# Three of eight k tiles of the state-space output projection as fp32r products of high and low parts

## The reference, cut to what matters

```python
y = ys.transpose(1, 0, 2, 3) + D[None, None, :, None] * xh
y = y.reshape(b, l, D_INNER)                      # D_INNER = 1024
y = y * jax.nn.silu(z)                            # the gated output
y = y * jax.lax.rsqrt(jnp.mean(y * y, axis=-1, keepdims=True) + EPS) * norm_w
return y @ W_out.T                                # 1024 -> 512, the output projection
```

## Time and profile before

| | |
|---|---|
| median of 3 runs | 2111.36 us (2105.56, 2112.68, 2111.36) |
| profiled execution, its own time | 2112.64 us |
| its span in the trace | 2110.9 us |
| state-space stage | about 0 to 905 us of the span |
| PE, DVE, ACT, POOL busy over the span | 94%, 69%, 58%, 18% |
| TensorE clock granted, mean | 0.972 of full speed |

### The profile page before, as it was taken

The page is one execution under the profiler, slowest core; times in us unless marked ns, Lnnn a source line. Parts: engine busy times, 40 slices in busy tenths (PEclk is TensorE's granted clock), DMA queues, the critical chain, the costliest instruction groups (busy, mean ns, idle before and its releaser), DMA issues. The chain is left out here.

```text
span 2110.9 us, 40225 instructions
## 1 busy us (share of the span) xinstructions
PE 1974.6 (94%) x13484; PEld 1328.5 (63%) x13484; DVE 1453.8 (69%) x2889; ACT 1221.2 (58%) x3068; POOL 390.2 (18%) x597
## 2 busy tenths in 40 slices
PE   7899999999999999858999999999999999889988
PEld 5667675768676767444565656656656655478853
DVE  7978787878787878526667575757575767556438
ACT  4435353534444444217878787878787787546614
POOL 1110101111111111231221222222222122100006
PEclk9999999999999999878999999999999999999999
DMA  7122222222222222242324343433333332631157
GB/s 215 49 69 70 60 79 60 79 60 79 55 83 50 89 50 68 80 125 63 109 70 118 76 122 81 121 81 102 93 102 96 88 98 73 180 133 61 60 188 270
DMA packets 120291, 200.72 MB, mean 95 GB/s; under 512 B 23072, under 2 KB 44576, under 8 KB 120096
## 3 DMA queue, kind: packets, MB, share of 16 engines
q1 hardware_dynamic: 110880, 179.20, 28.3%
q0 software_dynamic: 9216, 18.89, 3.6%
HBM read 117.27 MB, written 29.88 MB: 70 GB/s over the span
## 5 line engine op out<-in xcount | busy, mean ns | idle before, releaser
L1769 ACT ACTIVATE a_shared<-a_shared,a_mx 128x512 f32<-128x512 f32 x512 | 340.9, 669 | 57.3 <-DVE a_mx L1830 57.2
L1762 ACT ACTIVATE a_probs<-a_scores 128x512 f32<-128x512 f32 x512 | 291.7, 603 | 98.8 <-PE a_scores L1972 96.4
L1830 DVE TENSOR_REDUCE a_mx<-a_shared 128x1 f32<-128x512 f32 x512 | 318.4, 682 | 14.4 <-PE a_shared L1956 13.3
L1972 PE MATMUL a_scores<-a_qs,a_ks 98*128 98x512 f32 x512 | 218.9, 435 | 21.7 <-ACT a_probs L1762 17.4
L1956 PE MATMUL a_shared<-a_ks,a_qs 96*128 96x512 f32 x512 | 214.9, 431 | 18.9 <-ACT a_shared L1769 14.3
L939 PE MATMUL m_proj<-m_xt_hi,link 128*128 128x512 f32 x544 | 224.6, 413 | 6.3 <-DVE m_acc L652 6.3
L1094 PE MATMUL m_outp<-m_wout,m_g 128*128 128x512 f32 x512 | 225.2, 598 | 2.7 <-issue 2.7
L940 PE MATMUL m_proj<-m_xt_lo,link 128*128 128x512 f32 x544 | 215.4, 396 | 0.0
L941 PE MATMUL m_proj<-m_xt_hi,link 128*128 128x512 f32 x544 | 214.3, 394 | 0.0
L1930 PE MATMUL a_shared<-link 128*128 128x512 f32 x768 | 190.6, 401 | 18.9 <-POOL a_ks L1702 15.7
L467 ACT ACTIVATE m_acc<-m_proj,m_cb,m_cw 128x512 f32<-128x512 f32 x72 | 58.1, 817 | 257.5 <-PE m_proj L941 257.3
(11 more groups left out here) (266 smaller groups left out, 3487.7 us busy)
## 6 DMA issues: line engine op xcount, KB each, us to landing
m_dec<-step_decay SPq DMA_DIRECT2D x64, 256.0 KB, 4.1
a_qs<-link SPq DMA_DIRECT2D x256, 64.0 KB, 2.1
m_ce<-run_decay SPq DMA_DIRECT2D x128, 112.0 KB, 3.5
a_ks<-a_k_hi POOLq DMA_DIRECT2D x192, 64.0 KB, 2.4
e_x<-x SPq DMA_DIRECT2D x11, 1024.0 KB, 5.6
m_xt_in<-x_t_in SPq DMA_DIRECT2D x8, 1024.0 KB, 8.3
m_x_tok<-x_in SPq DMA_DIRECT2D x8, 1024.0 KB, 5.5
x<-m_x_tok SPq DMA_DIRECT2D x32, 256.0 KB, 2.2
```

Of the source, the lines that this page charges most:

```text
L1762: act.activation(probs[:, n % 2, h, :], scores[t.score_bank(n, h)][:, :], ACT.Exp, scale=-1.0).then_inc(exp_ready, 1)
L1769: act.activation(scored[:, :], scored[:, :], ACT.Exp, scale=-1.0, bias=mx[:, i % 2, j, h:h + 1], accum_out=den[:, i, j, h:h + 1]).then_inc ...
L1830: dve.tensor_reduce(mx[:, i % 2, j, h:h + 1], bank(what)[:, :], AX.X, ALU.min).then_inc(mx_ready, 1)
L1972: pe.matmul(scores[t.score_bank(n, h)][:, :], ks[0:STACK + 2, t.slot(i), h, j * P:(j + 1) * P], qs[0:STACK + 2, t.slot(i), h, :], start=Tr ...
```

## The change

Tiles n = 0, 1, 2 (`SPLIT_TILES` = 3) of the projection are computed as three fp32r products each, in the manner of `in_proj`; tiles 3 to 7 stay fp32. For that:

- PE: `out_proj` issues 9 fp32r products and 5 fp32 ones for each t, where there were 8 fp32 ones. It also waits once for `sq_used` of the third tile.
- ACT: in `squares`, a copy of the product to `g_hi` (fp32r) ahead of the square of tiles 0, 1, 2. A wait in `z_silus` for groups 2 and 3 (tiles 4, 5, 6), since the product of tiles 0 to 2 now lies in `zs`, whose buffer the gate is written to. The first square of all waits for the weight's preparation.
- POOL: in `sum_squares`, `low_part` for tiles 0, 1, 2: product minus `g_hi`, written to `g_lo` as fp32r. At the start, nine instructions more for the weight's parts (three multiplies, three copies, three subtractions of 128 x 512), and the multiply of `wout` over five tiles in place of eight.
- DVE: the same instructions; for tiles 0 to 2 `skip_added` writes into `xc` and `gated` into `zs`.
- SP: chunk 0 of the input weight is staged in `zs`, chunk 1 in `g`, chunk 2 in `xc`, the last in `g`'s end; the wait for `w_used` 3 goes, and `wout` is loaded by four DMAs in place of one, three of them into `sq` and `ssum`.

```diff
-        wout = sb("wout", [P, XT_TILES, DM])
+        wout = sb("wout", [P, XT_TILES - SPLIT_TILES, DM])
+        wout_hi = sb("wout_hi", [P, SPLIT_TILES, DM], F32R)
+        wout_lo = sb("wout_lo", [P, SPLIT_TILES, DM], F32R)
...
+        raw_wout = [sq[:, 0, :], sq[:, 1, :], ssum[:, :]]
+        def skipped(gr, j):
+            n = 2 * gr + j
+            return xc[:, gr % 2, j, :] if n < SPLIT_TILES else g[:, n - SPLIT_TILES, :]
+        def product(gr, j):
+            n = 2 * gr + j
+            return zs[:, gr % 2, j, :] if n < SPLIT_TILES else g[:, n - SPLIT_TILES, :]
...
-        places = [g_flat[:, 0:wide], *(g_flat[:, wide + n * narrow:wide + (n + 1) * narrow] for n in range(2)),
+        places = [zs_flat[:, 0:wide], g_flat[:, 0:narrow], late_xc,
                   *(dec_flat[:, n * narrow:(n + 1) * narrow] for n in range(4)),
-                  g_flat[:, wide + narrow:wide + 2 * narrow]]
+                  g_flat[:, (XT_TILES - SPLIT_TILES) * SEQ - narrow:(XT_TILES - SPLIT_TILES) * SEQ]]
...
-                for c in range(3, len(CHUNKS) - 1):
+                for c in range(3, len(CHUNKS)):
                     load_columns(c)
-                sp.wait_ge(w_used, DEC_CHUNK)
-                load_columns(len(CHUNKS) - 1)
...
-                sp.dma_start(wout[:, :, :], woutT.rearrange("(c p) n -> p c n", p=P)).then_inc(w_in[0], 16)
+                sp.dma_start(wout[:, :, :], woutT[SPLIT_TILES * P:DI].rearrange("(c p) n -> p c n", p=P)
+                             ).then_inc(w_in[0], 16)
+                for n in range(SPLIT_TILES):
+                    sp.dma_start(raw_wout[n], woutT[n * P:(n + 1) * P]).then_inc(w_in[0], 16)
...
             pool.wait_ge(m_ready, 1)
+            for n in range(SPLIT_TILES):
+                ins = pool.tensor_tensor(raw_wout[n], raw_wout[n], nw[:, n:n + 1].to_broadcast([P, DM]), ALU.mult)
+            ins.then_inc(const, 1)
+            pool.wait_ge(const, SET + 1)
+            for n in range(SPLIT_TILES):
+                ins = pool.tensor_copy(wout_hi[:, n, :], raw_wout[n])
+            ins.then_inc(const, 1)
+            pool.wait_ge(const, SET + 2)
+            for n in range(SPLIT_TILES):
+                ins = pool.tensor_tensor(wout_lo[:, n, :], raw_wout[n], wout_hi[:, n, :].bitcast(F32), ALU.subtract)
+            ins.then_inc(const, 1)
...
+            def low_part(gr, j):
+                n = 2 * gr + j
+                pool.tensor_tensor(g_lo[:, n, :], product(gr, j), g_hi[:, n, :].bitcast(F32), ALU.subtract)
...
+                        low_part(gr, j)
                         pool.tensor_copy(ssum[:, :], sq[:, 0, :]).then_inc(sq_used, 1)
...
+                        if n < SPLIT_TILES:
+                            low_part(gr, j)
                         pool.tensor_tensor(ssum[:, :], ssum[:, :], sq[:, j, :], ALU.add).then_inc(sq_used, 1)
...
             def z_silus(b, gr):
                 for j in range(2):
+                    if gr >= 2 and 2 * (gr - 2) + j < SPLIT_TILES:
+                        act.wait_ge(sq_used, at(b, XT_TILES, 2 * (gr - 2) + j + 1))
...
+                    if n < SPLIT_TILES:
+                        if n == 0 and not first:
+                            act.wait_ge(out_done, at(b, TT, 0))
+                        act.activation(g_hi[:, n, :], product(gr, j), ACT.Copy)
                     if n >= 2 or not first:
                         act.wait_ge(sq_used, at(b, XT_TILES, n - 1))
-                    act.activation(sq[:, j, :], g[:, n, :], ACT.Square).then_inc(sq_ready, 1)
+                    elif n == 0:
+                        act.wait_ge(const, SET + 3)
+                    act.activation(sq[:, j, :], product(gr, j), ACT.Square).then_inc(sq_ready, 1)
...
-                for k in range(XT_TILES):
-                    ins = pe.matmul(outp[t % 2][:, :], g[:, k, t * P:(t + 1) * P], wout[:, k, :],
-                                    start=(k == 0), stop=(k == XT_TILES - 1))
+                tile = slice(t * P, (t + 1) * P)
+                for k in range(SPLIT_TILES):
+                    for n, (gp, wp) in enumerate(((g_hi, wout_hi), (g_hi, wout_lo), (g_lo, wout_hi))):
+                        pe.matmul(outp[t % 2][:, :], gp[:, k, tile], wp[:, k, :], start=(k == n == 0), stop=False)
+                for k in range(XT_TILES - SPLIT_TILES):
+                    ins = pe.matmul(outp[t % 2][:, :], g[:, k, tile], wout[:, k, :],
+                                    start=False, stop=(k == XT_TILES - SPLIT_TILES - 1))
```

More of the change, by code:

```diff
@@ L111 @@
 LINK = 2 * KT * COLS
+SPLIT_TILES = 3
 SOFT_SCALE = (DM // 16) ** -0.5
@@ L180, in mamba_stage @@
         st = sb("st", [P, NC - 1, 2, HP])
-        g = sb("g", [P, XT_TILES, SEQ])
+        g = sb("g", [P, XT_TILES - SPLIT_TILES, SEQ])
+        g_hi = sb("g_hi", [P, SPLIT_TILES, SEQ], F32R)
+        g_lo = sb("g_lo", [P, SPLIT_TILES, SEQ], F32R)
         sq = sb("sq", [P, 2, SEQ])
@@ L190, in mamba_stage @@
         g_flat = g[:, :, :].rearrange("p a b -> p (a b)")
+        zs_flat = zs[:, :, :, :].rearrange("p s j n -> p (s j n)")
+        late_xc = xc[:, 1].rearrange("p j n -> p (j n)")
+        raw_wout = [sq[:, 0, :], sq[:, 1, :], ssum[:, :]]
[5 more added lines that the diff above has]
+            return zs[:, gr % 2, j, :] if n < SPLIT_TILES else g[:, n - SPLIT_TILES, :]
         dec_flat = dec[:, :, :, :].rearrange("p s h n -> p (s h n)")
@@ L267, in mamba_stage @@
         N_SMALL = 8
-        W_OUT_IN = 32
+        W_OUT_IN = 16 + 16 * (1 + SPLIT_TILES)
         raw = [xt_in[:, :, :], *(dec[:, 2 * n:2 * n + 2].rearrange("p g h n -> p (g h n)")
@@ L428, in _ @@
             pool.wait_ge(m_ready, 1)
-            pool.tensor_tensor(wout[:, :, :], wout[:, :, :], nw[:, :].unsqueeze(2).to_broadcast([P, XT_TILES, DM]),
+            for n in range(SPLIT_TILES):
[9 more added lines that the diff above has]
+            ins.then_inc(const, 1)
+            pool.tensor_tensor(wout[:, :, :], wout[:, :, :],
+                               nw[:, SPLIT_TILES:].unsqueeze(2).to_broadcast([P, XT_TILES - SPLIT_TILES, DM]),
                                ALU.mult).then_inc(const, 1)
+            pool.wait_ge(const, SET + 3)
+            def low_part(gr, j):
+                n = 2 * gr + j
+                pool.tensor_tensor(g_lo[:, n, :], product(gr, j), g_hi[:, n, :].bitcast(F32), ALU.subtract)
             def sum_squares(b, first, gr):
@@ L436, in sum_squares @@
                         squares = value(pool, at(b, XT_TILES, 1))
-                        met(pool, const, SET)
+                        met(pool, const, SET + 3)
                         pool.wait_ge(sq_ready, squares)
@@ L770, in skip_added @@
                     dve.wait_ge(out_done, at(b, TT, 0))
-                dve.scalar_tensor_tensor(out=g[:, n, :], in0=xc[:, gr % 2, j, :], scalar=dcol[:, n:n + 1],
+                dve.scalar_tensor_tensor(out=skipped(gr, j), in0=xc[:, gr % 2, j, :], scalar=dcol[:, n:n + 1],
                                          in1=yp[j][:, :], op0=ALU.mult, op1=ALU.add).then_inc(y_read, 1)
@@ L778, in gated @@
                     dve.wait_ge(y_read, at(b, XT_TILES, n + 1))
-                    dve.tensor_tensor(g[:, n, :], g[:, n, :], zs[:, gr % 2, j, :], ALU.mult).then_inc(g_ready, 1)
+                    dve.tensor_tensor(product(gr, j), skipped(gr, j), zs[:, gr % 2, j, :], ALU.mult).then_inc(g_ready, 1)
             def norm_scale(b):
@@ L1085, in out_proj @@
                 if t == 0:
-                    pe.wait_ge(const, SET + 1)
+                    pe.wait_ge(const, SET + 4)
+                    pe.wait_ge(sq_used, at(b, XT_TILES, SPLIT_TILES))
                     pe.wait_ge(g_ready, at(b, XT_TILES, XT_TILES))
```

## The result

| | before | after |
|---|---|---|
| median, 19 runs each | 2111.66 us | 2104.99 us |
| ratio, 95% interval | | 0.9973 [0.9966, 0.9980] |
| profiled execution, its own time | 2112.64 us | 2108.24 us |
| its span in the trace | 2110.9 us | 2106.5 us |

The account below looks back on a forecast made before the run. PE was taken as nearly the bound, with an equally long chain through ACT, DRAM and DVE. Passages -4.6, last sequence -2.0, first sequence +3 and +1 sum to -2.6 us, giving 2109 us, range 2098 to 2118.

Parts of the forecast that it names:

- The steady passage: Between sequences, DVE no longer waits 0.31 and 0.35 us for PE; seven passages gain 7 x 0.66 = 4.6 us.
- PE's saving: In `out_proj`, three fp32r products replace each fp32 one for tiles 0 to 2: 0.5 us per token tile, 2.0 per sequence.
- Rival C: In `out_proj`, fp32r products miss their 0.232 us step; at 0.29 us no gain, 2115 us; chance 0.06.
- PE's idle time at the z tile of group two: In a steady sequence, PE's wait for the convolution there grows from 0.55 to about 1.9 us.
- The last sequence: With no next sequence between its projections, DVE waits for PE each time, so the whole 2.0 us comes through.
- The first sequence: At the start, where DVE is the bound, POOL's longer preparation costs +3 us and low parts of tiles 0 and 1 +1.
- A, PE as the bound: Across the sequences, PE's 15.8 us come through nearly whole, 2096 to 2100 us; chance 0.30, of which 0.12 whole gain.
- B, the lock held through POOL's whole run: At `ce` in group two, POOL shuts DVE out, 1.3 us per sequence; 2117 to 2119 us likely; chance 0.18.

Follow-up runs that it names:

- e1_one_product: Changed kernel with only the high x high product for tiles 0 to 2, the two other products left out; 2109.66 us, 1.0000 to the kernel before.
- e5_late_scale: Changed kernel with POOL's multiply of `wout` moved behind the sums of group two of the first sequence; 2101.27 us, 0.9965 to the kernel before.
- e4_no_low: Changed kernel without POOL's subtractions for `g_lo`, the third product taking `g_hi` again; 2105.41 us, 0.9975 to the kernel before.
- e6_late_gap: Changed kernel with POOL's `wout` multiply late and `apply_norm` moved between group zero's two convolutions; 2098.77 us, 0.9948 to the kernel before.
- e3_split2: Changed kernel with two split tiles in place of three; 2121.82 us, 1.0058 to the kernel before.
- e12_split2_waits: Kernel with two split tiles, plus two long-met waits on PE ahead of each projection token tile; 2112.35 us, 1.0017 to the kernel before.
- e2_split1: Changed kernel with one split tile in place of three; 2117.13 us, 1.0035 to the kernel before.

## Why the prediction was right, and where not

The forecast (2109.0 us, 2098 to 2118, inside 0.3% the likeliest) held: 0.27% faster. The mechanism held in the passages, but the closeness of the sum is in part luck. In the traces the stage gives -4.7 - 0.9 + 2.8 = -2.8 us where I had -4.6 - 2.0 + 4 = -2.6, with two errors of about 1.1 us that cancel; and the 5.7 us of the ratio are twice that, with some 3 us that no term of mine covers. Step by step:

- **The steady passage.** Right in mechanism and size. The waits of 0.31 and 0.35 us of the earlier trace rows are gone, DVE's wait for the decays stands at 4.31 us (4.3 to 4.8 over the passages, 4.1 to 4.7 before), and seven passages give 4.7 us where I had 7 x 0.66 = 4.6. `e1_one_product` shows that PE's further work is not on the path.
- **PE's saving.** Right. Predicted 0.50 us per token tile. From its first start to the transposes behind it, the stretch of three took 20.71 us (347.16 to 367.87) and takes 19.18 (348.66 to 367.84): 0.51 us saved on each. The middle tile alone, 6.35 us (354.73 to 361.08) against 8 x 0.865 = 6.92, shows 0.57, since its first product, behind an fp32 one, shows 0.40 us more than I had and its five in fp32 0.44 less; the last tile, with 6.76 us, makes that up. Rival C is out.
- **PE's idle time at the z tile of group two** was to grow to 1.9 us. Wrong: it stayed at 0.55. PE meets the chain earlier, in group zero, where `carried_outputs` now waits for the states that DVE writes (0.20 us at 385.13). The passage to 422.48 is 1.0 us shorter than its like before (106.27 against 107.26 us); the other 1.0 of PE's 2.05 us is taken up by starts that come later: 0.36 us ahead of z tile 0, 0.26 between `local_outputs` and `carried_outputs` of group zero and 0.40 in the latter.
- **The last sequence**, "the whole 2.0 comes through": mis-sized, it gave 0.9. Token tiles 1 to 3 gave their 1.5 us, but the first one runs while PE's clock is low after its idle time ahead of it. The windows of the kernel before and then of the changed one:

```profile
865.00:870.00 5.00, 4.79 (x7) 2.20 (x8) 0.11 (x1) 4.48 (x4) 2.53 (x2) 0.58 0.98 369
```

```profile
865.00:870.00 5.00, 5.00 (x11) 3.07 (x10) 0.00 (x0) 3.34 (x3) 1.06 (x1) 0.54 0.62 224
870.00:875.00 5.00, 5.00 (x21) 3.12 (x20) 0.16 (x1) 1.16 (x1) 0.98 (x1) 1.00 0.01 3
```

  I had costed the tile from rows at full clock. It lasted 8.92 us before (865.21 to 874.13) and 9.32 after (863.47 to 872.79): it began 1.7 us earlier, but the clock came back at 869.6, hardly other than at 869.2 before, so more of the tile ran at the low clock, which ate its saving. The last 0.2 us lie between `xdt` and the tile.
- **The first sequence**, +3 for the preparation and +1 for the low parts: +2.8 measured at PE's wait for `xdt`. Preparation 2.2, in another place than I had worked out (the scans; `e5_late_scale` gives 3.4 back); casts and subtractions 2.1, of which the low parts are 1.2 (`e4_no_low`); and two gains that I had not priced, 0.7 from the decays that land earlier and 0.8 of slack in group two.
- **The rest** is 1.6 us behind the stage in the one pair of traces; the medians differ by more than the spans do, and I leave it open.
- **Rivals.** A, PE as the bound: refuted by `e1_one_product`. B, the lock held through POOL's whole run: refuted by `ce` at 414.15, which took 1.09 us between two POOL instructions with no wait of POOL's to help it (413.00 + 1.30 is 414.30, and the next began at 414.25). A wide range was right for another reason than I gave: variants close to this one lie 0.25% under it (`e6_late_gap`) and 0.85% over it (`e3_split2`), by the order on DVE, by a fetch and by the DVE instruction that POOL's long multiply catches, none of which I had priced.

## What to carry to other kernels

Two chains of nearly equal length can make an edit look worthless alone: shorten the engine that is busiest, then look at the order on the one that waits, since `apply_norm`'s move paid only after PE had room. Don't give an engine more slack than its partner can use, for TensorE idling 2.1 us and more ahead of its work lost its full clock here (it kept it with 1.6 us and less), and the partner then waited for it. And where a variant is slower by the same amount in every loop passage with no work to explain it, look at when small stores on the critical path land, and at what else is on the DMA engines then, instruction fetches among it. A long GpSimd instruction beside a busy VectorE is worth moving: what it catches changed with each variant's start.

## What the runs showed of the hardware

- In 18 loop passages in which a packet of 16 KB of instructions began 0.7 to 1.7 us behind the issue of a 32 KB store of short packets, the store landed after 2.9 to 3.7 us and not 1.9. It repeated in each pass of the loop, and two more instructions per token tile moved it (`e12_split2_waits`: 1.9 to 2.4 us).
- DVE got its turn between two POOL instructions that follow each other (`ce`, 1.09 us at 414.15), and POOL's next two took 3.55 us in place of 2.73. The Trainium skill ("SBUF — State Buffer", Who interferes with whom) has the lock go to whoever starts first, for one instruction; these rows agree, and show it changing hands inside a row of back-to-back work.
- A scan, too, stood for a POOL instruction: 5.92 us for four in place of 2.44. A cast (5.56 us in `e2_split1`) and `ce` (6.19 us in `e3_split2`) stood longer still.
- The granted clock, a mix of the levels of 1.2 and 2.4 GHz, fell to 0.71, 0.78 and 0.66 in windows of 10 us with an idle stretch of 3.75, 2.55 and 2.09 us on TensorE, and stayed at 1.00 with 1.61 and 1.19 us.
- An fp32r product that follows one in fp32 starts its successor 0.63 us later, and not 0.23, while the five fp32 ones ahead of the next such switch show 0.44 us less. Over three tiles it evens out: 6.39 us each, where 9 x 0.232 + 5 x 0.865 gives 6.41.
